# Local similarities in the pre-activation convolution chain: norms' rows in 8 transfers of twelve rows, batches of products in halves

## The chip, the cores and the metric

The kernel runs on one core of a Trainium2 chip. The metric is the device time of one execution in microseconds (us). The engines are named as in the profile: PE (matrix products), DVE (vector), ACT (scalar), POOL (GpSimd), SP (the queue that issues most transfers). ACTq and SPq are the queues in which ACT and SP issue transfers; 16 DMA engines carry them.

## The reference, cut to what matters

The input is 32 images of 32 channels, 56x56 pixels. Four residual stages follow each other, each on the input normalised per channel. The change lies in the second, local similarities:

```python
K, PAD, EPS = 5, 2, 1e-08
patches = _extract_patches(x)                       # 25 shifted copies, zero padded
dot = jnp.einsum('bchw,bckhw->bkhw', x, patches)    # product with each shift, summed over channels
norm_x = jnp.sqrt(jnp.sum(x * x, axis=1))
norm_p = jnp.sqrt(jnp.sum(patches * patches, axis=1))
sim = dot / jnp.maximum(norm_x[:, None] * norm_p, EPS)
weight = (sim + 1.0) * 0.5 * spatial_weight[None, :, None, None]
out = jnp.einsum('bckhw,bkhw->bchw', patches, weight)
```

The third stage is a gate per channel, and the fourth sorts, convolves and attends.

## The kernel before, in words

**Groups and rounds.** Four images with their 32 channels fill the 128 partitions: a group. The eight groups pass through a pipeline of rounds, from about 215 us to 2090 us of the span (the rest of the kernel isn't touched). In one round `a_vector` weighs and adds the shifts for group k ("taps"), and beside it `a_end_vector` finishes the group before, and `a_start_vector` prepares the next one: normalises it, makes the products of each pixel with its shifted neighbours, and turns them into similarities. The first round has no taps, the second has taps and a start but no end, six rounds (a hardware loop of three times two) have all three, and two last rounds start nothing. So eight rounds start a group. A round ends at a barrier of all engines (`end_round`, `close_round`), which SP closes.

**Steps.** By symmetry only 12 shifts (`HALF_TAPS`) are computed. With the centre there are 13 taps, and each image is done in two halves of 28 rows, so a round has 26 steps n. In step n DVE makes two weighted copies of the half image (L672, L676; `a_g`), PE adds them into PSUM with 8 + 8 products of 128x128 by 392 columns (L759, L763; `a_acc`), and DVE may be two steps ahead: step n waits for PE's step n - 2. The weights come back from DRAM (`simd`): for each step SP issues four loads (L520), each spreading one row over 32 partitions, into one of three buffers; the load for step n is issued when DVE has used the buffer, mostly after its step n - 3. After step 12 DVE reads the PSUM half out (L686), which PE's step 13 waits for, and after step 25 the other half.

**What a start does beside the steps.** DVE's step 5 normalises. ACT squares (L732), PE sums the squares over channels with 28 small products (L788) in its step 7, and ACT takes the root. DVE turns this into inverse norms in step 10 (L644 to L648, waits `a_nrm`, sets `a_nt`). PE transposes the two small results (L798) in its step 12, behind that step's dots, ACT copies them out (L746; `a_rt`), and then ACT issues the writes of the norms to `rnd` and `simd` (L704, L705), waits for them, and issues the loads of the norms' rows: for each of the 12 shifts one load into `rnc` (the norms) and one into `sim` (the norms shifted), each of 4 rows (one for each image) of 3136 floats, 24 loads in all (L711, L712; `a_rnl`). DVE's step 16 waits for all of them, multiplies (L654) and takes the similarity of the first half (L627, `a_sh`), which ACT stores (L720).

**Batches.** The products are made in six batches q: three for each half image (t = q modulo 3), each with four shifts j (`prd[0]` to `prd[3]`, DVE L619, 4 instructions). PE sums them over channels in `dots(q)` (L772, 32 products into PSUM). There is one set of `prd` buffers, so batch q waits for dots(q - 1) (`a_dot`). Before, batches 0 and 1 stand in steps 8 and 9, batch 2 in step 12, batches 3, 4 and 5 in steps 17, 18 and 20, similarities in steps 16 and 22, on PE the dots in the same steps.

Shift number m = 3j + t is in row 32j + 4t + image of `rnc` and `sim`.

Of the kernel before, what the change touches and what calls it, by code (L numbers as in the profile page):

```python
# [15 lines left out]
B, C, H, W = 32, 32, 56, 56  # L16
N = H * W
P = 128
TB = P // C
# [164 lines left out]
        assert not touched(first) & touched(ROW_LOTS[q - 1][1])  # L184
IMG_NET, IMG_PAIRS = placed(network(H))
TMP = max(max(n for _, _, n in ROW_NET), W * max(n for _, _, n in IMG_NET))
HALF_TAPS = [(0, 1), (0, 2)] + [(dh, dw) for dh in (1, 2) for dw in range(-2, 3)]


def tap(dh, dw):  # L190
# [3 lines left out]
def program(nc, x, wdct_t, keep, ident_in, same_batch, same_head, shifts, sw, gate_w, temp,  # L194
# [4 lines left out]
    with ctx:  # L199
# [7 lines left out]
        rnd = nc.dram_tensor("rnd", (TB * N + P,), f32).ap()  # L207
# [246 lines left out]
        a_tp, a_rt, a_rnw, a_rnl, a_sst = (sem(n, early) for n in ("a_tp", "a_rt", "a_rnw", "a_rnl", "a_sst"))  # L454
# [47 lines left out]


        PLACE = [n % 3 for n in range(2 * NS - 2)] + [1, 2]
        BEFORE = [max((m for m in range(n) if PLACE[m] == PLACE[n]), default=None) for n in range(2 * NS)]
        TURN = [max(m for m in range(2 * NS) if PLACE[m] == i) for i in range(3)]

# [15 lines left out]
        def a_sync(sp, end, start, k, taps=True, more=True):  # L523

            def end_out():
                sp.wait_ge(a_x3, 1)
                sp.dma_start(x3_t[end], xt[1 - k]).then_inc(a_st3, 16)

            def xp_out():
                sp.wait_ge(a_xp, 1)  # L530
                sp.dma_start(xpad_t[end], xp).then_inc(a_stp, 16)

            if start is not None:
                sp.dma_start(rnc, x_t[start]).then_inc(a_x, 16)
                for b in range(TB):
                    sp.dma_start(yt[C * b:C * b + 2, :], ydct_t[start, b]).then_inc(a_y, 16)
            for n in range(2 * NS):
                if taps and n >= 3:
                    sp.wait_ge(a_g, BEFORE[n] + 1)
                    s_load(sp, k, n)  # L540
                if end is not None and n == 8:
                    end_out()
                if end is not None and n == 10:
                    xp_out()
            if more:
                if start is not None:
                    sp.wait_ge(a_sst, 16 * 2 * NJ)
                for n in range(3):
                    if taps:
                        sp.wait_ge(a_g, TURN[n] + 1)  # L550
                    s_load(sp, 1 - k, n)
            if start is not None:
                sp.wait_ge(a_x, 16)
                sp.wait_ge(a_y, 16 * TB)
            if end is not None:
                sp.wait_ge(a_st3, 16)
                sp.wait_ge(a_stp, 16)
# [51 lines left out]
        def a_start_vector(chain, o, n):  # L609

            dve, link = chain.dve, chain.link

            def batch(q):
                h, t = divmod(q, NT3)
                if q:
                    dve.wait_ge(a_dot, q)
                for j in range(NJ):
                    dh, dw = HALF_TAPS[NT3 * j + t]
                    last = nc.vector.tensor_tensor(img3(prd[j]), rect(xn[o], HH * h + R1, HH, 0, 0),  # L619
                                                   rect(xn[o], HH * h + R1, HH, dh, dw), ALU.mult)  # L620
                last.then_inc(a_pr, 1)

            def similarity(h):
                dve.wait_ge(a_dot, NT3 * (h + 1))
                for i in range(4):
                    c = slice(HN * h + 392 * i, HN * h + 392 * i + 392)
                    last = nc.vector.scalar_tensor_tensor(out=sim[:, c], in0=sim[:, c], scalar=1e8,  # L627
                                                          in1=psum[:, 4 + i, 0:392], op0=ALU.min, op1=ALU.mult)
                last.then_inc(a_sh, 1)

            if n == 3:
                dve.wait_ge(a_x, 16)
                dve.wait_ge(a_y, 16 * TB)
                link(nc.vector.tensor_tensor(rnc, rnc, yt, ALU.add))
            if n == 4:
                chain.moments(rnc)
            if n == 5:
                chain.normalise(xi[o], rnc).then_inc(a_norm, 1)
                dve.wait_ge(a_norm, 1)
            if n in (8, 9):  # L640
                batch(n - 8)
            if n == 10:
                dve.wait_ge(a_nrm, 1)
                link(nc.vector.tensor_scalar_max(nr, nr, 1e-18))  # L644
                link(nc.vector.reciprocal(nr, nr))
                newton(link, nr, n2, nt)
                link(nc.vector.tensor_tensor(nt, nr, nr, ALU.mult))
                nc.vector.scalar_tensor_tensor(out=nt, in0=nt, scalar=1e8, in1=n2, op0=ALU.min,  # L648
                                               op1=ALU.mult).then_inc(a_nt, 1)
            if n == 12:  # L650
                batch(2)
            if n == 16:
                dve.wait_ge(a_rnl, 16 * 2 * NH)
                link(nc.vector.tensor_tensor(sim, rnc, sim, ALU.mult))  # L654
                similarity(0)
            if n in (17, 18):
                batch(n - 14)
            if n == 20:
                batch(5)
            if n == 22:  # L660
                similarity(1)

        def a_vector(dve, k, beside):

# [36 lines left out]
        def rn_scalar(act, k):  # L701

            act.wait_ge(a_rt, 2)
            act.dma_start(rnd[0:TB * N].rearrange("(r n) -> r n", n=TC), nrt).then_inc(a_rnw, 16)  # L704
            act.dma_start(simd[1 - k, NH].rearrange("b (k n) -> (b k) n", n=TC), ntt).then_inc(a_rnw, 16)  # L705
            act.wait_ge(a_rnw, 32)
            act.wait_ge(a_xc, 1)
            images = rnd[0:TB * N].rearrange("(b n) -> b n", n=N)
            for m, (dh, dw) in enumerate(HALF_TAPS):
                at = C * (m // NT3) + TB * (m % NT3)  # L710
                act.dma_start(rnc[at:at + TB, :], images).then_inc(a_rnl, 16)  # L711
                act.dma_start(sim[at:at + TB, :],  # L712
                              rnd[W * dh + dw:W * dh + dw + TB * N].rearrange("(b n) -> b n", n=N)).then_inc(a_rnl, 16)

        def sim_scalar(act, k):

            for h in range(2):
                act.wait_ge(a_sh, h + 1)
                for j in range(NJ):
                    act.dma_start(simd[1 - k, NT3 * j:NT3 * j + NT3, :, HN * h:HN * h + HN].rearrange("t b n -> (t b) n"),  # L720
                                  sim[C * j:C * j + ROWS_J, HN * h:HN * h + HN]).then_inc(a_sst, 16)
            act.wait_ge(a_sst, 16 * 2 * NJ)
# [28 lines left out]
        def a_tensor(pe, taps, ends, starts):  # L751
# [14 lines left out]

            def dots(q):
                t = q % NT3
                pe.wait_ge(a_pr, q + 1)
                for i in range(4):  # L770
                    for j in range(NJ):
                        last = nc.tensor.matmul(psum[C * j:C * j + C, 4 + i, 0:392], sel[:, t, :],  # L772
                                                prd[j][:, 392 * i:392 * i + 392], start=(t == 0), stop=(t == NT3 - 1),
                                                tile_position=(0, C * j))
                last.then_inc(a_dot, 1)

            for n in range(2 * NS):
# [6 lines left out]
                if starts:  # L784
                    if n == 7:
                        pe.wait_ge(a_sq, 1)
                        for i in range(NB):
                            last = nc.tensor.matmul(n2p.rearrange("p (b k) -> p b k", b=TB)[:, :, i],  # L788
                                                    sim[:, TC * i:TC * i + TC], ones4[:, 0::C], start=True, stop=True)
                        last.then_inc(a_n2, 1)  # L790
                        pe.wait_ge(a_n2e, 1)
                    if n in (8, 9):
                        dots(n - 8)
                    if n == 12:
                        dots(2)
                        pe.wait_ge(a_nt, 1)
                        for p, v in ((turnp[0], nr), (turnp[1], nt)):
                            last = nc.tensor.transpose(p, v, ident[0:TC, 0:TC])  # L798
                        last.then_inc(a_tp, 1)
                        pe.wait_ge(a_rt, 2)  # L800
                    if n == 17:
                        pe.wait_ge(a_sh, 1)
                    if n in (17, 18):
                        dots(n - 14)
                    if n == 20:
                        dots(5)

        def a_init(dve):

# [1218 lines left out]
```

## Time and profile before

| what | value |
|---|---|
| median of 3 runs | 15069.19 us (15061.56 to 15069.54) |
| profiled execution, its own time | 15071.54 us |
| its span, first to last instruction | 15070.0 us |
| mean granted PE clock | 0.713 of full speed |
| DVE busy over the span | 13765.0 us (91%) |
| DMA wait in front of L654, all 8 starts | 204.9 us |

The span is the time between the first and last instruction; 1.5 us lie around it. "Idle" is the time an engine stood still before an instruction, and the arrow names what ended it.

### The profile page before, as it was taken

How to read it: one execution, taken by the hardware profiler on the slowest of the kernel's cores; microseconds unless marked ns; L12 is line 12 of the kernel's file. 1: busy time of each engine (PE TensorE's matmuls, PEld its weight loads, DVE VectorE, ACT ScalarE, POOL GpSimd, SP SyncE). 2: the span in 40 equal slices, each digit the busy share in tenths (PEclk: the TensorE clock that was granted, in tenths of full speed). 3: DMA queues.
4: the chain of work that ended last, by engine and by line, in shares of the span. 5: the costliest groups of instructions: out<-in, count | busy, mean ns of one | idle time of the engine just before them, and what ended most of it. 6: DMA issues, size and time to landing. Idle time of an engine off the chain costs nothing. (4 is left out here: it accounts for less than half of the span.)

```text
span 15070.0 us, 121660 instructions
## 1 busy us (share of the span) xinstructions
PE 6719.5 (45%) x42188; PEld 2750.0 (18%) x42188; DVE 13765.0 (91%) x8241; ACT 7124.7 (47%) x6595; POOL 6003.7 (40%) x4372
## 2 busy tenths in 40 slices
PE   4777746480026525625714813833832015433310
PEld 2443422120012112211211201211211002111100
DVE  4777778899999999999999999999999999989978
ACT  0000013355565575565565566566566555444443
POOL 0000000066666666666666666666666640000000
PEclk8888878795558757857956956966866557666655
DMA  1455543210001001000100100100100001221232
GB/s 39 117 136 127 126 111 77 58 37 12 12 12 35 27 11 36 26 12 31 31 12 30 32 12 25 37 12 13 44 17 12 33 30 51 86 66 55 77 76 66
DMA packets 343162, 699.24 MB, mean 46 GB/s; under 512 B 71581, under 2 KB 275582, under 8 KB 331702
## 3 DMA queue, kind: packets, MB, share of 16 engines
q1 hardware_dynamic: 337398, 675.91, 16.6%
q10 hardware_dynamic: 5120, 15.26, 0.5%
q8 instruction: 342, 5.60, 0.2%
q14 instruction: 302, 2.47, 0.1%
HBM read 480.98 MB, written 209.95 MB: 46 GB/s over the span
## 5 line engine op out<-in xcount | busy, mean ns | idle before, releaser
L1197 DVE COPY_PREDICATED arena<-psum,arena 128x4096 f32<-128x4096 uint32 (+26 forms) x1456 | 4009.7, 2771 | 46.3 <-ACT psum L1157 45.9
L1204 DVE COPY_PREDICATED arena<-psum,arena 128x4096 f32<-128x4096 uint32 (+26 forms) x1456 | 3971.4, 2744 | 42.0
L1023 PE MATMUL psum<-arena,wt 128*32 128x448 f32 x31360 | 3217.1, 572 | 1248.2 <-DMA arena<-xpad 697.1
L1122 POOL TENSOR_TENSOR arena<-arena 128x1024 int32<-128x1024 int32 (+26 forms) x1456 | 2077.8, 1433 | 3063.7 <-DVE arena L1189 3060.3
L1108 POOL TENSOR_TENSOR arena<-arena 128x1024 bf16<-128x1024 f32 (+26 forms) x1456 | 1975.4, 1363 | 3223.7 <-SPq L267 3021.4
L1145 ACT ACTIVATE arena<-arena 128x4096 f32<-128x4096 f32 (+26 forms) x1456 | 3071.5, 2126 | 70.6 <-DVE arena L1204 37.9
L1165 ACT ACTIVATE masks<-psum 128x512 fp8e4<-128x512 f32 (+27 forms) x1256 | 923.1, 736 | 3566.7 <-DVE arena L1204 3565.5
L1114 POOL TENSOR_TENSOR arena<-arena 128x1024 int32<-128x1024 int32 (+26 forms) x1456 | 2005.7, 1384 | 0.0
L1023 PEld LDWEIGHTS psum<-arena,wt 128*32 128x32 f32 x31360 | 1038.2, 115 | 3429.7 <-issue 2321.6
L1413 PE MATMUL psum<-ident,arena 128*112 128x128 f32 x896 | 197.1, 385 | 2441.6 <-ACT arena L1332 1880.7
L1189 DVE TENSOR_TENSOR arena<-arena 128x1024 f32<-128x1024 f32 (+26 forms) x1456 | 1164.2, 813 | 99.7 <-POOL arena L1114 99.7
L1647 ACT ACTIVATE arena<-arena 128x2048 f32<-128x2048 f32 (+28 forms) x364 | 767.1, 2124 | 871.0 <-DVE arena L1680 869.2
L1682 DVE COPY_PREDICATED arena<-arena 128x2048 f32<-128x2048 uint8 (+28 forms) x364 | 974.0, 2692 | 76.5 <-ACT arena L1647 76.4
L1680 DVE COPY_PREDICATED arena<-arena 128x2048 f32<-128x2048 uint8 (+28 forms) x364 | 969.9, 2680 | 10.0
L1157 ACT ACTIVATE psum<-arena 128x512 f32<-128x512 bf16 (+10 forms) x1248 | 912.5, 731 | 0.0
L759 PE MATMUL psum<-arena 128*128 128x392 f32 x1664 | 669.7, 551 | 366.2 <-DVE arena L676 345.0
L1724 PE MATMUL psum<-masks,arena 128*128 128x512 fp8e4 (+3 forms) x992 | 326.5, 506 | 1104.0 <-DMA masks<-row_masks 633.8
L1457 PE MATMUL psum<-ident,arena 128*128 128x128 f32 x256 | 71.0, 433 | 1594.0 <-DVE arena L1391 1594.0
L1469 PE MATMUL psum<-arena 128*128 128x392 f32 x1024 | 572.2, 727 | 210.1 <-ACT arena L1324 78.8
L1413 PEld LDWEIGHTS psum<-ident,arena 128*112 128x112 f32 x896 | 155.1, 199 | 2498.7 <-ACT arena L1332 1891.7
L699 ACT ACTIVATE small<-small 128x1 f32<-128x1 f32 x24 | 4.9, 203 | 1209.4 <-DVE small L576 1209.4
L763 PE MATMUL psum<-arena 128*128 128x392 f32 x1536 | 543.3, 495 | 0.0
(132 smaller groups left out, 7662.0 us busy)
## 6 DMA issues: line engine op xcount, KB each, us to landing
arena<-xpad SPq DMA_DIRECT2D x896, 108.5 KB, 2.3
arena<-simd SPq DMA_DIRECT2D x416, 210.0 KB, 4.3
arena<-simd SPq DMA_DIRECT2D x416, 196.0 KB, 4.2
xpad<-arena SPq DMA_DIRECT2D x8, 1924.0 KB, 8.0
arena<-in_x SPq DMA_DIRECT2D x8, 1568.0 KB, 7.7
x3d<-arena SPq DMA_DIRECT2D x8, 1568.0 KB, 5.2
prodd<-arena SPq DMA_DIRECT2D x8, 1568.0 KB, 5.1
arena<-prodd SPq DMA_DIRECT2D x8, 1568.0 KB, 13.5
```

Of the source, the lines that this page charges most:

```text
L1023: last = nc.tensor.matmul(psum[C * b:C * b + C, n % C_BANKS, 0:CROWS * W], wt[:, g, C * w:C * w + C], cx[i % 2][b][:, y0:y0 + CROWS, x0:x0 ...
L1108: last = nc.gpsimd.tensor_tensor(packed_view(dbuf, here, piece, 1), lo, hi, ALU.subtract)
L1114: last = nc.gpsimd.tensor_tensor(packed_view(stmp, here, piece, 1), lo, hi, ALU.add)
L1122: last = nc.gpsimd.tensor_tensor(hi, packed_view(stmp, here, piece, 1), lo, ALU.subtract)
L1145: last = nc.scalar.activation(packed_view(ptmp, here, piece, NP), pair_views(pay[b], piece, NP)[0], ACT.Copy)
L1157: nc.scalar.activation(pmask[:, at:at + n], dbuf[:, here:here + n], ACT.Relu).then_inc(d_mw[k], 1)
L1165: last = nc.scalar.activation(masks[:, q % 4, lo:hi].bitcast(mybir.dt.float8e4), pmask[:, at:at + hi - lo], ACT.Sign, saturate=False)
L1189: last = nc.vector.tensor_tensor(lo, lo, hi, ALU.min)
L1197: last = nc.vector.copy_predicated(lo, wide_mask(q, k, piece, here), hi)
L1204: last = nc.vector.copy_predicated(hi, wide_mask(q, k, piece, here), packed_view(ptmp, here, piece, NP))
L1680: last = nc.vector.copy_predicated(hi, mask, packed_view(utmp, here, piece, NP))
L1682: last = nc.vector.copy_predicated(lo, mask, hi)
```

## The change

1. The order of `HALF_TAPS` changes, so that the three shifts of each j lie at equal distances. The loads of one j then go in one transfer of twelve rows, for `rnc` and for `sim`: 8 transfers. The source is a hand-written pattern, outermost three shifts (a step of 0 for `rnc`, of 56 or 1 floats for `sim`), then four images, then 3136 floats.
2. The inverse norms are computed in DVE's step 9, and PE transposes them in its step 9, ahead of dots(0).
3. A batch is made in two halves of two instructions in two steps (`BATCH`), and its dots come in the second of them. Similarities are in steps 16 and 23; step 15 has the wait for the norms' rows and L654.
4. SP's first three loads for the next round wait only for the stores of the first half of the similarities, and ACT's second four stores wait for the first four.

```diff
-HALF_TAPS = [(0, 1), (0, 2)] + [(dh, dw) for dh in (1, 2) for dw in range(-2, 3)]
+HALF_TAPS = [(dh, dw) for dw in (1, 2) for dh in range(3)] + [(dh, dw) for dh in (1, 2) for dw in range(-2, 1)]
...
+        BATCH = [(8, 9), (10, 11), (13, 14), (16, 17), (18, 19), (20, 21)]
+        SIMILAR = [16, 23]
...
-                    sp.wait_ge(a_sst, 16 * 2 * NJ)
+                    sp.wait_ge(a_sst, 16 * NJ)
...
-            def batch(q):
+            def batch(q, half):
...
-                for j in range(NJ):
+                for j in range(NJ // 2 * half, NJ // 2 * half + NJ // 2):
...
-            if n in (8, 9):
-                batch(n - 8)
-            if n == 10:
+            if n == 9:
                 dve.wait_ge(a_nrm, 1)
...
-            if n == 12:
-                batch(2)
-            if n == 16:
-                dve.wait_ge(a_rnl, 16 * 2 * NH)
+            if n == 15:
+                dve.wait_ge(a_rnl, 16 * 2 * NJ)
                 link(nc.vector.tensor_tensor(sim, rnc, sim, ALU.mult))
...
+            if n in SIMILAR:
+                similarity(SIMILAR.index(n))
+            for q, pair in enumerate(BATCH):
+                for half in range(2):
+                    if n == pair[half]:
+                        batch(q, half)
...
-            for m, (dh, dw) in enumerate(HALF_TAPS):
-                at = C * (m // NT3) + TB * (m % NT3)
-                act.dma_start(rnc[at:at + TB, :], images).then_inc(a_rnl, 16)
-                act.dma_start(sim[at:at + TB, :],
-                              rnd[W * dh + dw:W * dh + dw + TB * N].rearrange("(b n) -> b n", n=N)).then_inc(a_rnl, 16)
+            for j in range(NJ):
+                (dh, dw), (nh, nw) = HALF_TAPS[NT3 * j:NT3 * j + 2]
+                for dst, first, move in ((rnc, 0, 0), (sim, W * dh + dw, W * (nh - dh) + nw - dw)):
+                    act.dma_start(dst[C * j:C * j + ROWS_J, :],
+                                  bass.AP(rnd.tensor, rnd.offset + first, [[move, NT3], [N, TB], [1, N]])).then_inc(a_rnl, 16)
...
+                if h:
+                    act.wait_ge(a_sst, 16 * NJ)
...
-                pe.wait_ge(a_pr, q + 1)
+                pe.wait_ge(a_pr, 2 * q + 2)
...
-                    if n in (8, 9):
-                        dots(n - 8)
-                    if n == 12:
-                        dots(2)
+                    if n == 9:
                         pe.wait_ge(a_nt, 1)
                         for p, v in ((turnp[0], nr), (turnp[1], nt)):
                             last = nc.tensor.transpose(p, v, ident[0:TC, 0:TC])
                         last.then_inc(a_tp, 1)
                         pe.wait_ge(a_rt, 2)
...
+                    for q, (_, half) in enumerate(BATCH):
+                        if n == half:
+                            if q == NT3:
+                                pe.wait_ge(a_sh, 1)
+                            dots(q)
```

## Rows read from the trace of the kernel before

**Rows 1.** The page's first part: busy time, share, instructions of each engine.
```profile
PE 6719.5 (45%) x42188; PEld 2750.0 (18%) x42188; DVE 13765.0 (91%) x8241; ACT 7124.7 (47%) x6595; POOL 6003.7 (40%) x4372
```
**Rows 2.** Groups of instructions, 948.9 to 1173.8 us: busy, mean ns | idle before, releasers.
```profile
L672 DVE SCALAR_TENSOR_TENSOR arena<-arena 128x1568 f32<-128x1568 f32 x26 | 46.5, 1787 | 13.7 <-PE psum L763 8.2 <-issue 5.5
L772 PE MATMUL psum<-arena 128*32 128x392 f32 x192 | 17.0, 495 | 3.1 <-DVE arena L619 3.1
```
**Rows 3.** Line L654: duration ns min/median/max, first and last start; idle before it.
```profile
L654 DVE TENSOR_TENSOR arena<-arena x8: 3424/3424/3426, 300.0 to 1842.5; 128x3136 f32<-128x3136 f32 x8
  DMA arena<-rnd: 204.9, 8
```
**Rows 4.** Timeline of DVE, one loop round: start, us, instruction [idle before <-releaser].
```profile
1086.03 6.89 DVE L619 TENSOR_TENSOR arena<-arena 128x1568 f32<-128x1568 f32 x4
...
1102.98 6.90 DVE L619 TENSOR_TENSOR arena<-arena 128x1568 f32<-128x1568 f32 x4 [6.65 <-PE psum L772]
...
1113.20 0.21 DVE L644 TENSOR_SCALAR arena<-arena 112x112 f32<-112x112 f32 x1
...
1115.57 0.28 DVE L648 SCALAR_TENSOR_TENSOR arena<-arena 112x112 f32<-112x112 f32 x1
...
1173.84 3.42 DVE L654 TENSOR_TENSOR arena<-arena 128x3136 f32<-128x3136 f32 x1 [26.28 <-DMA arena<-rnd]
```
**Rows 5.** Timeline of PE in the same round.
```profile
1091.74 5.59 PE L759 MATMUL psum<-arena 128*128 128x392 f32 x8 [0.35 <-ACT arena L741]
1097.12 3.02 PE L763 MATMUL psum<-arena 128*128 128x392 f32 x8
...
1130.58 0.41 PE L798 MATMUL psum<-ident,arena 112*112 112x112 f32 x2
...
1138.53 2.79 PE L759 MATMUL psum<-arena 128*128 128x392 f32 x8
1141.16 2.80 PE L763 MATMUL psum<-arena 128*128 128x392 f32 x8
```
**Rows 6.** Timeline of ACT and its queue in the same round.
```profile
1131.02 0.42 ACT L746 ACTIVATE arena<-psum 112x112 f32<-112x112 f32 x2 [39.01 <-PE psum L798]
...
1136.95 0.25 ACTq L711 DMA_DIRECT2D arena<-rnd  x1
...
1144.84 0.32 ACTq L712 DMA_DIRECT2D arena<-rnd  x1
```
**Rows 7.** DMA queues, 305.3 to 310 us: four stores of twelve rows (6272 bytes).
```profile
DMA packets 96, 0.30 MB, mean 64 GB/s; under 512 B 48, under 2 KB 48, under 8 KB 96
```
**Rows 8.** DMA queues, 279 to 299 us: the row loads of the first round.
```profile
DMA packets 192, 1.21 MB, mean 61 GB/s; under 512 B 95, under 2 KB 95, under 8 KB 95
```
**Rows 9.** DMA queues, 1137 to 1153 us: row loads (q10) beside step loads (q1).
```profile
DMA packets 530, 2.54 MB, mean 159 GB/s; under 512 B 180, under 2 KB 180, under 8 KB 498
```
**Rows 10.** DMA queues, 1157 to 1169 us: DVE waits, and nothing new is issued.
```profile
DMA packets 151, 0.82 MB, mean 69 GB/s; under 512 B 65, under 2 KB 65, under 8 KB 109
q10 hardware_dynamic: 83, 0.53, 15.2%
q1 hardware_dynamic: 68, 0.30, 10.1%
```
**Rows 11.** Timeline of the first round (no taps), and L654 of the second.
```profile
247.62 4.48 PE L772 MATMUL psum<-arena 128*32 128x392 f32 x32 [0.35 <-ACT arena L741]
...
275.97 0.40 PE L798 MATMUL psum<-ident,arena 112*112 112x112 f32 x2
...
299.99 3.42 DVE L654 TENSOR_TENSOR arena<-arena 128x3136 f32<-128x3136 f32 x1 [28.44 <-DMA arena<-rnd]
...
347.43 5.41 SPq L520 DMA_DIRECT2D arena<-simd  x12
...
355.31 1.79 DVE L672 SCALAR_TENSOR_TENSOR arena<-arena 128x1568 f32<-128x1568 f32 x1 [12.39 <-SPq L267]
...
498.97 3.43 DVE L654 TENSOR_TENSOR arena<-arena 128x3136 f32<-128x3136 f32 x1 [27.45 <-DMA arena<-rnd]
```

More of the change, by code:

```diff
@@ L649, in a_start_vector @@
                                                op1=ALU.mult).then_inc(a_nt, 1)
-            if n == 12:
-                batch(2)
-            if n == 16:
-                dve.wait_ge(a_rnl, 16 * 2 * NH)
+            if n == 15:
+                dve.wait_ge(a_rnl, 16 * 2 * NJ)
                 link(nc.vector.tensor_tensor(sim, rnc, sim, ALU.mult))
[L655 to L661, printed above, removed]
+            if n in SIMILAR:
[4 more added lines that the diff above has]
+                        batch(q, half)
         def a_vector(dve, k, beside):
@@ L707, in rn_scalar @@
             act.wait_ge(a_xc, 1)
-            images = rnd[0:TB * N].rearrange("(b n) -> b n", n=N)
-            for m, (dh, dw) in enumerate(HALF_TAPS):
-                at = C * (m // NT3) + TB * (m % NT3)
-                act.dma_start(rnc[at:at + TB, :], images).then_inc(a_rnl, 16)
-                act.dma_start(sim[at:at + TB, :],
-                              rnd[W * dh + dw:W * dh + dw + TB * N].rearrange("(b n) -> b n", n=N)).then_inc(a_rnl, 16)
+            for j in range(NJ):
[3 more added lines that the diff above has]
+                                  bass.AP(rnd.tensor, rnd.offset + first, [[move, NT3], [N, TB], [1, N]])).then_inc(a_rnl, 16)
         def sim_scalar(act, k):
@@ L800, in a_tensor @@
                         pe.wait_ge(a_rt, 2)
[L801 to L806, printed above, removed]
+                    for q, (_, half) in enumerate(BATCH):
[3 more added lines that the diff above has]
+                            dots(q)
         def a_init(dve):
```

## The prediction, made before the changed kernel ran

> **What bounds the kernel now.** I read the page first: DVE is busy for 13765 of 15070 us [rows 1], so only DVE's own stops, or work taken off it, are worth anything. The change takes no instruction off DVE. Next the groups of instructions of one loop round: DVE's copies L672 have waited 8.2 us for PE in all [rows 2]. The line view then finds the one large stop: L654, the product with the norms' rows, has waited 204.9 us for the loads from `rnd`, 8 times, 25.6 us a time [rows 3]. The timelines of a round show why. PE transposes the norms at 1130.6, ACT issues the loads from 1136.95 to 1145.2, and DVE, idle for 26.3 us, goes on at 1173.84 [rows 4 to 6]. So the loads take 36.9 us from the first issue, 28.7 us after the last one. The issues themselves aren't the bound.
>
> **Why the loads are slow.** A packet view counts data rows and small closing packets. The 24 loads of the first round leave 96 rows and some 95 packets under 512 B, four for each load [rows 8]; the four stores of twelve rows leave 48 and 48, twelve for each [rows 7]. So a transfer closes once on each engine it uses, and four-row loads use four of 16, always few at once: q10 and q1 together hold 15.2 + 10.1 = 25.3% of 16 engines, four of them, full, while DVE waits [rows 10]. Each of the four carries 24 rows. In the first round, alone, that takes from 279 to 299.99, less 1.3 us for start and landing, 19.7 us or 0.82 us a row [rows 8, 11]. From 1137 to 1153 there are 530 - 498 = 32 rows, 8 an engine, 2.0 us each, beside 498 - 180 = 318 rows of step loads, 20 an engine [rows 9]. From 1157 to 1169 there are 42 rows, 10.5 an engine, 1.14 us each, beside 44 rows of step loads that four engines still owe, one for one [rows 10]. A few engines with two queues are the bottleneck.
>
> **The change, part by part.** I put it on the clock of this round.
>
> *Norms earlier.* DVE now makes half of batch 0 in step 8 (2 x 1.7 = 3.4 us, half of 6.9, from 1086.0 to 1089.4), step 9's copies to 1092.9, then the norms (2.6 us, from L644 at 1113.20 to the end of L648 at 1115.8 [rows 4]) and the other half. PE's sums of squares end at 1091.4, step 8's accumulation takes 8.2 us at the lower clock and step 9's 5.3 (2 x 2.63) [rows 5]: 1105.2, transposes 1105.7, copies out by 1106.2, where it was 1131.4 [rows 6]. Norms leave 25.2 us earlier. With the same 5.5 us for the write [rows 6], the loads are issued from 1111.7, the first row starts near 1112.3.
>
> *Where DVE asks for them.* dots(0) now come behind the transposes and end at 1109.0 (2.8 us, 17.0 / 6) [rows 2], so half 1 of batch 1 waits 5.6 us and step 10's copies 1.2 us for the accumulation; batch 1 had waited 6.65 us [rows 4]. Then DVE goes on in steps of 3.4 + 3.4 us: step 11 to 1119.5, step 12 to 1121.2, the half read-out waits 2.0 us for PE's step 12 and ends at 1129.1, steps 13 and 14 end at 1139.3, step 15's copies at 1142.7. There L654 stands now. The rest (17 us of products, similarities, PE-bound last steps) is the same work; the halves of batches 4 and 5 wait 1.6 us each for dots, two waits of 1.9 to 2.2 us in steps 15 and 16 go. Over the round the small waits grow by 12.2 - 11.4 = 0.8 us. If no row load were late, a loop round would save its stop less that: the six have (204.9 - 28.4 - 27.4) / 6 = 24.8 (the second round's is 27.4) [rows 3, 11], so 24.0, and the second 26.6.
>
> *8 transfers for 24.* 16 issues of 0.35 us go from ACT's queue [rows 6], where nothing waits for them: nothing. What counts is engines. The destination still counts twelve rows outermost, but the new source counts three shifts outermost. In the rows above the number of engines equals the outermost count of both sides, four and twelve [rows 7, 8]; no transfer of the trace has sides that differ. Equal shares along both outermost counts give three engines, and I take that; twelve is the other bound. On three, 96 rows are 32 an engine, not 24. The packing thus makes the loads longer.
>
> The Trainium skill, "DMA: Bandwidth & Descriptors" ("Why a DMA increments its semaphore by 16 and not by 1"), says that a transfer is cut over the largest number of engines up to 16 that divides the outermost counts of both sides, and its rules for kernel authors warn of a small outermost dimension. By that rule it is three here, and the four and twelve above agree.
>
> *The wait that is left.* There are 1142.7 - 1112.3 = 30.4 us for 32 rows. Lower bound, the rate of the first round without step loads: 32 x 0.82 = 26.2 us, hidden. Upper bound, the rates of the round itself: DVE doesn't stop now, so step loads come on (five between 1112 and 1143, 40 rows an engine, as dense as before), 15 rows at 2.0 us, and 17 at 1.14 once DVE stands: 19.4 us, landed at 1161.9, a wait of 19.2 us. The step loads are there, so I stay near the upper: 16 us, a little less because a share now closes once for four rows. A part of it may show as DVE's copies (L672) waiting for a late step load, since three engines hold those up too; it is the same time.
>
> *First round.* No step loads, no taps. PE's sums end before 247.6, so norms from 248, transposes at 251 for 275.97 [rows 11], loads from 253.7; 26.2 us, landed at 280.6 where it was 300.0: 19 us. At its end SP's 12 loads (5.4 us, 347.43) stood between the last stores and the barrier [rows 11]; they now wait for first-half stores only: 5 us. In full rounds the same wait was covered by PE-bound steps. Together 24 us.
>
> *Sum.* 24 + (26.6 - 16) + 6 x (24.0 - 16) = 83 us. The profiled execution took 15071.5 us (1.5 around the span), 2.3 above the median of the runs. 15071.5 - 83 = 14988.5, by the median 14986.
>
> **Rivals.**
> *Hidden (0.20).* The rows go over twelve engines, or four rows in a line go so much faster that 30.4 us are enough. For: the stores of twelve rows did use twelve engines [rows 7]. 24 + 26.6 + 6 x 24 = 195 us saved, 14874. The skill page's rules also say to put many small transfers into one large one; by that rule this rival would win, but the row loads' time lies behind the last issue [rows 4, 6], which speaks against issue cost.
> *Slower or no gain (0.08).* The step-load rows queued on the three engines keep all 32 rows at 2.0 us [rows 9]: 64 us, landed at 1176.3, a wait of 33.6 us in seven rounds, 24 - 7 - 6 x 9.6 = 41 us lost, 15110. It decides from a wait of 195 / 7 = 27.8 us, or 1.8 us a row. Against: the rate was 1.14 as soon as DVE stood [rows 10].
> *The forecast (0.72):* exposed by 5 to 23 us.
>
> **How the numbers follow.** What this measurement can tell from no change is about 0.2%, 30 us. The upper bound above gives 24 + 7.4 + 28.8 = 60 us saved, 15009; if the dense rate outlasts DVE's stop by some 8 us, 3.5 us more in each of seven rounds, near 15030. The lower end takes in the hidden case, 14874 less a few: 14866. Within that range I see 0.9; the forecast's own range is 14915 to 15030. Savings under 30 us need a wait above 23.5 us, all in the second rival: same 0.05, slower 0.03, faster 0.92.
>
> **What would show it.** In the packet view of a round's row loads: 24 closing packets for 96 rows (96 if twelve engines). L798 some 25 us earlier in the round. L654 still waiting for `rnd` in seven rounds, about 16 us, nearly none in the first; or L672 waiting for DMA from `simd` in step 15. With twelve engines no wait at L654 at all. A gain in the first round unlike 24 us, or new waits for L772 above 1.6 us, would say that my steps are misplaced.

## The result, and the profile after

The changed kernel takes 14888.53 us (median of 4 runs, 14887.01 to 14903.87), the kernel before 15068.69 (4 runs beside it): ratio 0.9884, 95% interval 0.9867 to 0.9901. It is faster by 180 us, where 83 were forecast; that lies 97 us below the forecast and 14.5 us above the time of the first rival (hidden, 14874). The profiled execution took 14887.01 us.

The page's first part, engine by engine:

```profile
span 14884.8 us, 121541 instructions
PE 6707.4 (45%) x42188; PEld 2746.4 (18%) x42188; DVE 13771.3 (93%) x8241; ACT 7130.0 (48%) x6595; POOL 6008.9 (40%) x4372
```

DVE does the same work (13771 us against 13765 in [rows 1]) in a span 185 us shorter: the whole gain is idle time of DVE. The line view of L652, which was L654 [rows 3], says whose:

```profile
L652 DVE TENSOR_TENSOR arena<-arena x8: 3415/3418/3420, 278.3 to 1644.6; 128x3136 f32<-128x3136 f32 x8
its engine sat idle before it (us, times) until:
who waited for it (us, times):
```

Nothing stands between the second line and the third: all eight waits for `rnd`, 204.9 us before, are gone. Nor did they turn into late step loads. DVE's copies (L669, before L672) waited for `simd` 9.1 us in the whole kernel:

```profile
L669 DVE SCALAR_TENSOR_TENSOR arena<-arena x208: 1781/1791/1795, 329.8 to 1864.6; 128x1568 f32<-128x1568 f32 x104
its engine sat idle before it (us, times) until:
  PE psum L761: 82.8, 48
  SPq L267: 21.0, 6
  issue: 11.1, 2
  DMA arena<-simd: 9.1, 7
```

The same loop round as in [rows 4], by DVE's timeline (start, us, instruction, [idle before <-releaser]):

```profile
984.31 3.48 DVE L621 TENSOR_TENSOR arena<-arena 128x1568 f32<-128x1568 f32 x2
...
991.12 0.21 DVE L644 TENSOR_SCALAR arena<-arena 112x112 f32<-112x112 f32 x1
...
1007.33 3.49 DVE L621 TENSOR_TENSOR arena<-arena 128x1568 f32<-128x1568 f32 x2 [5.28 <-PE psum L770]
...
1025.49 1.98 DVE L683 TENSOR_TENSOR arena<-arena,psum 128x392 f32<-128x392 f32 x4 [2.04 <-PE psum L757]
...
1031.84 1.79 DVE L669 SCALAR_TENSOR_TENSOR arena<-arena 128x1568 f32<-128x1568 f32 x1 [0.96 <-DMA arena<-simd]
...
1042.06 3.42 DVE L652 TENSOR_TENSOR arena<-arena 128x3136 f32<-128x3136 f32 x1
```

PE and ACT's queue in it, answering to [rows 5, 6]:

```profile
1003.55 0.36 PE L793 MATMUL psum<-ident,arena 112*112 112x112 f32 x2
1004.42 2.84 PE L770 MATMUL psum<-arena 128*32 128x392 f32 x32 [0.51 <-ACT arena L744]
```
```profile
1003.95 0.42 ACT L744 ACTIVATE arena<-psum 112x112 f32<-112x112 f32 x2 [13.35 <-PE psum L793]
...
1008.67 3.59 ACTq L708 DMA_DIRECT2D arena<-rnd  x5
```

From the start of the first batch to the transposes it is 1003.55 - 984.31 = 19.2 us (1130.58 - 1086.03 = 44.6 before): 25.3 us earlier in the round, 25.2 were forecast. From the first issue of a row load to L652 it is 33.4 us, in which DVE never stops for rows. An issue of the new form takes 3.59 / 5 = 0.72 us, not 0.35, and nothing waited for it.

Now the engines. In the first round nothing but row loads runs, and the queue view from 254 to 271 us answers to [rows 8]:

```profile
DMA packets 116, 1.19 MB, mean 70 GB/s; under 512 B 21, under 2 KB 21, under 8 KB 21
q10 hardware_dynamic: 116, 1.19, 17.5%
```

95 rows and 21 closing packets, where the kernel before had 95 of the latter. (24 closings are due, three for each of 8 transfers; the window cuts some off.) The queue's 17.5% of 16 engines is 2.8 engines busy all through. So the transfers run on three engines, as forecast, with 32 rows each. The packet records of q10 give the time from the first row's start to the last row's end:

| | rows / closings an engine | first round, alone | beside step loads |
|---|---|---|---|
| before, 24 transfers | 24 / 24 | 19.6 us | 34.6 to 36.6 us |
| after, 8 transfers | 32 / 8 | 16.0 us | 26.1 to 27.3 us |

More rows on fewer engines were faster. The records also give each packet's own duration. In the first round a row lasts 0.73 us on average before and 0.50 us after; beside step loads 0.85 to 0.95 before and 0.64 to 0.67 after. No row of any run is shorter than 0.47 us. A closing lasts 0.01 to 0.03 us on average in every run, at most 0.09. The queue views say the same of the rows: from 279 to 299 us of the kernel before, q10 holds 22.4% of 16 engines, 0.75 us for each of 96 rows, and 17.5% of 17 us above is 0.50 us for each of 95:

```profile
q10 hardware_dynamic: 191, 1.20, 22.4%
```

In the loop round the step loads pass at the same time: from 1009 to 1036 us the queue of step loads holds 39.0% of the 16 engines.

```profile
q1 hardware_dynamic: 530, 2.39, 39.0%
q10 hardware_dynamic: 115, 1.18, 14.7%
```

Last, the first round (start of what [rows 11] shows), with the late end of the round:

```profile
247.91 0.22 DVE L644 TENSOR_SCALAR arena<-arena 112x112 f32<-112x112 f32 x1 [10.70 <-ACT arena L741]
...
278.33 3.42 DVE L652 TENSOR_TENSOR arena<-arena 128x3136 f32<-128x3136 f32 x1
...
329.77 1.79 DVE L669 SCALAR_TENSOR_TENSOR arena<-arena 128x1568 f32<-128x1568 f32 x1 [6.94 <-SPq L267]
```

L652 starts at 278.33 here without a wait for rows. These had landed at 271.5, and what DVE waited for on the way were the norms (10.70 us above) and the dots (5.07 and 5.57 us before L621). The first L669 starts at 329.77 instead of 355.31: 25.5 us. The second round's stands at 519.29, 189.5 later (216.5 before): 27.0 us. The six loop rounds take 200.6 us each and took 223.8: 23.2 each, 139 in all. That makes 191.7. The first instruction of the next stage (L953, before L959) starts at 1929.0 instead of 2120.2, 191.2 us earlier. At the end of the span 185.2 are left; the missing 6 us arise in stages that the change doesn't touch and are smaller than the scatter of the runs.

### The profile page after: what moved, and what is told of

It reads as the page before. It is cut to its first block and busy times, and to the rows that moved or that the text cites. A ratio compares the mean times of both kernels' runs of the same rounds, so it can differ in the third digit from the quotient of the medians.

```text
span 14884.8 us, 121541 instructions
## 1 busy us (share of the span) xinstructions
PE 6707.4 (45%) x42188; PEld 2746.4 (18%) x42188; DVE 13771.3 (93%) x8241; ACT 7130.0 (48%) x6595; POOL 6008.9 (40%) x4372
```

## The experiments

Two theories of the gain stood after the result. **A:** a transfer closes with a packet on each engine it uses, that packet costs about as much as a row while step loads run, and 8 closings an engine for 24 is why 32 rows pass in 26.5 us. From 24 rows with 24 closings (35.1 us: 1.46 a pair) and 8 groups of four rows with one closing (26.5 us: 3.31 a group), a row costs (3.31 - 1.46) / 3 = 0.62 us and a closing 0.85; the experiments use 0.61 and 0.86. From 19.6 and 16.0 us of the first round, without step loads, the same equations give 0.39 and 0.42. This is a fit of two prices to two totals, and the packets' own durations above speak against it as a price of the closing packet; the runs below say how far it carries. **B:** the transfers' form matters little; the rows are hidden because the norms leave 25 us earlier. Later two more came up, on the halves of the batches: **C**, that they cost waits, and **D**, that they don't (experiment 5 gives both letters a narrower meaning).

The kernels of experiments 1 to 4 stand beside 12 runs of the kernel before (median 15073.42), those of 5 to 8 beside 9 others (15079.97). Between these groups, and with the changed kernel, ratios are compared, or the time at which the next stage begins in the trace.

**1. The changed kernel with 24 transfers of four rows again.**

```diff
-            for j in range(NJ):
-                (dh, dw), (nh, nw) = HALF_TAPS[NT3 * j:NT3 * j + 2]
-                for dst, first, move in ((rnc, 0, 0), (sim, ...)):
-                    act.dma_start(dst[C * j:C * j + ROWS_J, :], ...)
+            for m, (dh, dw) in enumerate(HALF_TAPS):
+                at = C * (m // NT3) + TB * (m % NT3)
+                act.dma_start(rnc[at:at + TB, :], images).then_inc(a_rnl, 16)
+                act.dma_start(sim[at:at + TB, :], ...).then_inc(a_rnl, 16)
```

> The changed kernel with the norms' rows in 24 loads of four rows again, all else as changed. Theory A (a load's closing packet on each engine is what made a row cost 1.5 us; in threes of engines with four rows to a closing it costs 0.8): the rows take some 35 us as before, DVE asks for them after some 31, so L652 waits about 4 to 5 us in seven rounds, 14889 + 32 = about 14920 us. Theory B (the row rate rose because the new order of the round leaves the DMA engines freer): 24 rows an engine at 0.82 us, 20 us, no wait, 14889 us.

Measured: 14932.95 us (14922.94 to 14952.25), ratio 0.9909 (0.9894 to 0.9924). The rows took 35 to 39 us, 22.6 in the first round, with 96 closings. The next stage begins at 1976.7 us, 47.7 later than in the changed kernel. The wait shows mostly where the prediction had said that a part of it might, at DVE's copies, though a step earlier: 6.43 us in step 14 of one loop round, not in step 15. L652 waits little, and the copies L669 wait for the step loads, which the same engines carry:

```profile
  DMA arena<-rnd: 4.4, 6
```
```profile
  PE psum L762: 82.7, 49
  DMA arena<-simd: 46.1, 13
```

(4.4 us is L652's line, the two others are L669's; in the changed kernel they were none, 82.8 and 9.1.) So B is wrong: packing is worth 48 us by the start of the next stage, and 40 by the medians, each set against the kernel before beside it. A had 14920, so the cost is somewhat above its number, and most of it falls on the step loads, for which DVE asks first.

**2. The kernel before with the 8 transfers alone**: the new `HALF_TAPS` and the new loads, nothing else.

> The kernel before with only the loads in 8 transfers of twelve rows (and the order of shifts that this needs). Theory A: the rows take 26 to 27 us after the first one instead of 35, L654 waits 8.7 us less in seven rounds and 3.6 less in the first, 15069 - 65 = about 15004 us. Theory B: three engines with 32 rows at 1.5 us, 48 us, the wait grows by 12 us a round, about 15155 us. Either way 24 closing packets for 96 rows.

Measured: 15032.56 us (15017.61 to 15038.78), ratio 0.9971 (0.9961 to 0.9982). The rows took 25.4 to 30.1 us, 16.2 in the first round, and L654 waits 155.9 us for them, 49 less than in [rows 3]; A had 15004, 29 us better, B 15155:

```profile
  DMA arena<-rnd: 155.9, 8
```

The next stage begins at 2078.1, 42 us earlier. My forecast was that packing on three engines makes the loads longer; here it stands alone and makes them shorter, in every round. With the packing worth 42 to 48 us in either kernel, the other 143 to 149 of the 191 us come with the rest of the change: experiment 1, which has everything but the packing, reaches the next stage 143.5 us before the kernel before. That rest is the earlier norms, the moved batches and SP's wait (experiment 6); no run has the earlier norms alone. It took both parts to bring the wait to nothing.

**3. The changed kernel with half-width rows**, 16 transfers for 8, the same three engines and bytes.

```diff
-                    act.dma_start(dst[C * j:C * j + ROWS_J, :],
-                                  bass.AP(..., [[move, NT3], [N, TB], [1, N]])).then_inc(a_rnl, 16)
+                    for c in (0, HN):
+                        act.dma_start(dst[C * j:C * j + ROWS_J, c:c + HN],
+                                      bass.AP(..., [[move, NT3], [N, TB], [1, HN]])).then_inc(a_rnl, 16)
```

> The changed kernel with each load of twelve rows cut into two of half the columns: 16 transfers, the same bytes, twice the closings (16 an engine) and twice the data packets (64 of 6272 bytes an engine). Theory A with closings alone: 8 more closings at some 0.86 us, rows done after 33 us, L652 waits 2 to 3 us in seven rounds, about 14907 us. If only the bytes count: unchanged 14889. If each packet, large or small, takes its turn with a step-load packet: some 45 us, a wait of 14 us, about 14990.

Measured: 14907.85 us (14900.91 to 14912.49), ratio 0.9889 (0.9874 to 0.9904). The rows took 31.7 to 34.7 us beside step loads, with 48 closings; 32 x 0.61 + 16 x 0.86 = 33.3 is what A gives. The bytes alone would have left 26.5, and a cost for each packet of any kind far more. L652 waits 28.6 us in all, and the next stage begins 21 us later:

```profile
  DMA arena<-rnd: 28.6, 7
```

By time alone the run wouldn't tell (the intervals of the ratios overlap); the packets and the wait do. Beside step loads A's two prices come out to within 1.6 us. In the first round, where nothing else runs, they don't: 32 x 0.39 + 16 x 0.42 = 19.2 us, and the half rows took 16.4, 0.4 more than the whole rows of the changed kernel (255 to 273 us):

```profile
DMA packets 240, 1.20 MB, mean 67 GB/s; under 512 B 48, under 2 KB 48, under 8 KB 240
q10 hardware_dynamic: 240, 1.20, 17.1%
```

So eight more closings an engine, and twice the packets, cost next to nothing alone and 7 us beside step loads. The run doubles three things at once (closings, row packets and transfers), so it can't give the 7 us to the closings. The records point elsewhere. Where q10's packet ends and no other of q10 starts at once, its engine has broken off from q10. In the changed kernel's loop rounds that happens after 35 to 44 of 96 rows and 9 to 13 of 24 closings; here after 67 to 88 of 192 and 20 to 24 of 48. (The records don't name the engine, so these counts go by the times alone.) The breaks double, and most of them stand behind rows. The step loads are denser here too, with 16 rows a us for 14.

**4. The changed kernel with whole batches.** The batches' dots had cost the changed kernel waits before L621 (25 of them), as they had the kernel before (81.3 us in 13):

```profile
L621 DVE TENSOR_TENSOR arena<-arena x192: 1781/1785/1794, 233.7 to 1692.6; 128x1568 f32<-128x1568 f32 x192
its engine sat idle before it (us, times) until:
  PE psum L770: 80.6, 25
```

```diff
-        BATCH = [(8, 9), (10, 11), (13, 14), (16, 17), (18, 19), (20, 21)]
+        BATCH = [(9, 9), (11, 11), (14, 14), (17, 17), (19, 19), (21, 21)]
```

> The changed kernel with each batch made whole in the second step of its pair (9, 11, 14, 17, 19, 21), dots and all else in the same steps. Theory C (the halves cost: half 0 of the next batch asks for dots one step too early, so DVE waits for PE): a schedule laid out from the rows gives 6 us a round less in seven rounds, about 14845 us; the wait of 5.3 us before step 10's half goes. Rival D (the halves spread DVE's work and so keep DVE and PE from waiting for each other): 10 to 40 us slower than the changed kernel, 14900 to 14930 us, with longer waits for L770.

Measured: 14836.98 us (14832.66 to 14845.18), ratio 0.9843 (0.983 to 0.9857), the next stage from 1888.7 us, 40.3 earlier.

```profile
L621 DVE TENSOR_TENSOR arena<-arena x192: 1778/1783/1794, 250.6 to 1652.7; 128x1568 f32<-128x1568 f32 x192
its engine sat idle before it (us, times) until:
  PE psum L770: 19.4, 4
```

61 us of waits before L621 went, and some came back: L652 waits 10.4 us for rows again, L644 for the norms 40.9 instead of 16.9. C holds for these places: the halved batches as placed cost 40 us against whole ones a step later by the start of the next stage, 52 to 56 by the medians. The dots need both halves, so a first half one step ahead brings PE nothing; it asks for the `prd` buffers a step sooner and waits there for the dots of the batch before (the 5.28 us above; at the same batch the whole version doesn't wait).

**5. Five batches whole, at later places.**

```diff
+        BATCH = [(9, 9), (11, 12), (14, 14), (18, 18), (20, 20), (22, 22)]
```

> The changed kernel with five of the six batches of products whole, at (9,9), (11,12), (14,14), (18,18), (20,20), (22,22). Theory C (a batch must lie where the shifted copy it displaces is not the one TensorE waits for; where a half costs VectorE a wait for TensorE, it is the place that costs, not the halving by itself): working out each round's order of waits from the durations of the profile after gives 9.7 us a round less than the changed kernel, over seven rounds 68 us, so 14820 us; the second batch stays in halves and must not bring the waits back. Theory D (whole batches gain because they are whole): five of six whole gives five sixths of the 51.5 us that six gave, so 14846 us.

Measured: 14860.72 us (14856.94 to 14864.28), ratio 0.9854 (0.9839 to 0.9869). C's 14820 is missed by 41 us. The next stage begins at 1900.6 us, 12 after that of experiment 4. Against experiment 4, DVE saves 20 us of waits at the read-outs L683 (43.1 for 62.8), and spends 23 more where the rows are due:

```profile
  DMA arena<-rnd: 33.8, 7
```

Here L652 is asked for earlier and the rows, in 27 to 30 us, bound it again; L669's waits for PE grew by 7 us as well. My working had taken the rows as hidden at a fixed time. D's arithmetic (14846) is nearer, but 20.2 us of waits are left before L621, about as with all six whole (19.4), though one batch is halved here; so nothing speaks for the halving as such being the cost. The schedule by places is no better than its row-load term.

**6. The changed kernel with SP's wait put back** (`sp.wait_ge(a_sst, 16 * 2 * NJ)`).

> The changed kernel with one thing put back: SyncE waits for all of the step's stores of the similarities, 16*2*NJ, before it loads on, and not for 16*NJ. If that wait is hidden behind the rows of norms, the time stays at 14889 us within 10. If it holds the first load of the next round's step, it costs up to 6 us in the first round and less in the others: 14894 to 14925 us.

Measured: 14901.44 us (14894.53 to 14905.61), ratio 0.9881 (0.9866 to 0.9896), no different from the changed kernel's. In the trace the second round starts its copies at 334.6 us, not 329.8: 4.8 us, as the first round's term had it (5). The next stage begins 18.9 us later in this one execution, with L669, L621 and L644 each waiting 2 to 8 us more; whether the loop rounds pay too stays open, since the runs don't show it.

**7. Norms still earlier.** The sums of squares two steps earlier on PE (n == 5), their root on ACT ahead of the copy of the normed rows, norms and transposes in step 8.

```diff
-        BATCH = [(8, 9), (10, 11), (13, 14), (16, 17), (18, 19), (20, 21)]
+        BATCH = [(7, 8), (10, 10), (12, 12), (18, 18), (20, 20), (22, 22)]
...
-            if n == 9:
+            if n == 8:
                 dve.wait_ge(a_nrm, 1)
...
-                    if n == 7:
+                    if n == 5:
                         pe.wait_ge(a_sq, 1)
...
-                    if n == 9:
+                    if n == 8:
                         pe.wait_ge(a_nt, 1)
```

> The changed kernel with the sums of squares two steps earlier on TensorE, their root on ScalarE ahead of the copy of the normed rows, the norms one step earlier on VectorE and TensorE, and the batches at (7,8), (10,10), (12,12), (18,18), (20,20), (22,22). Theory C, by the same working as for the late places: 1.4 us a round less than those, over seven rounds 10 us, so 14810 us, and the idle time of VectorE at the read of the norms (2.7 us a round in that working) gone. Rival: the sums meet TensorE while it is behind, and the time stays at that of the late places, 14820 us, or above.

Measured: 14824.55 us (14824.03 to 14830.65), ratio 0.9833 (0.9819 to 0.9846): the fastest of the study, 14.6 us above what C gave. L652 waits for nothing and L644 in the first round alone. The step loads pay part of it. The row loads now take 31.5 to 32.8 us with the same 32 rows and 8 closings an engine, where A gives 26.4; 17 rows of step loads a us start beside them, in the changed kernel 14:

```profile
  PE psum L761: 73.0, 34
  DMA arena<-simd: 43.1, 21
```

**8. The same with the norms written three times,** so that the four loads of `rnc` go over twelve engines, a row each.

```diff
-            act.dma_start(rnd[0:TB * N].rearrange("(r n) -> r n", n=TC), nrt).then_inc(a_rnw, 16)
+            for c in range(NT3):
+                act.dma_start(rnd[TB * N * c:TB * N * c + TB * N].rearrange(...), nrt).then_inc(a_rnw, 16)
...
+                act.dma_start(rnc[C * j:C * j + ROWS_J, :],
+                              rnd[0:NT3 * TB * N].rearrange("(r n) -> r n", n=N)).then_inc(a_rnl, 16)
```

> As the kernel with the sums early, but the norms are written three times, so that the four loads of rnc take rows on twelve engines, a row each; the four of sim stay on three. On those three engines 20 rows and 8 closings stand for 32 rows and 8 closings. Theory A (0.61 us a row and 0.86 us a closing beside the step loads): the last row lands after 19 us and not 26.5. If the rows are fully hidden already, the time is that of the kernel with the sums early, 14810 us, within 10; two more stores of 12 packets and 12 x 4 closings may cost the step loads up to 5 us. If the three loaded engines still hold the step loads up by a few us a round, it gains those: 14780 to 14800 us.

Measured: 14840.71 us (14835.07 to 14855.97), ratio 0.9841 (0.9827 to 0.9854). The rows land 6 us earlier than in experiment 7, after 25.5 to 28.2 us, with 60 closings, and not after 19. Nothing is gained: the next stage begins 20.1 us later than in experiment 7. DVE's timeline shows what a late load before the half's read-out does. At 1008.52 DVE waits for a step load, and then at 1021.53 for PE, whose step 13 had to wait for the read-out L683:

```profile
1008.52 1.79 DVE L669 SCALAR_TENSOR_TENSOR arena<-arena 128x1568 f32<-128x1568 f32 x1 [4.28 <-DMA arena<-simd]
...
1011.94 1.97 DVE L683 TENSOR_TENSOR arena<-arena,psum 128x392 f32<-128x392 f32 x4
...
1021.53 1.79 DVE L669 SCALAR_TENSOR_TENSOR arena<-arena 128x1568 f32<-128x1568 f32 x1 [4.22 <-PE psum L764]
```
```profile
1013.96 4.79 PE L760 MATMUL psum<-arena 128*128 128x392 f32 x8 [6.24 <-DVE arena L683]
```

L669's waits for PE are 101.0 us in all against 73.0, those for `simd` 35.0 against 43.1.

In its first round, alone, the rows took 16.9 us on twelve engines, where three took 16.0 to 16.4. The queue view from 255 to 273 us:

```profile
q10 hardware_dynamic: 156, 1.20, 32.5%
```

That is 5.2 engines busy on average instead of 2.8, for the same rows in the same time. Each row lasted 0.96 us on average, and up to 1.93.

**A's prices against all the rounds,** in us:

| kernel | rows / closings an engine | alone: A, measured | beside step loads: A, measured |
|---|---|---|---|
| 1, four-row loads | 24 / 24 | 19.4, 22.6 | 35.3, 35.0 to 39.4 |
| 2, packing alone | 32 / 8 | 15.8, 16.2 | 26.4, 25.4 to 30.1 |
| 3, half rows | 32 (as 64 halves) / 16 | 19.2, 16.4 | 33.3, 31.7 to 34.7 |
| 7, norms earlier | 32 / 8 | 15.8, 16.4 | 26.4, 31.5 to 32.8 |
| 8, twelve engines | 20 / 8 | 11.2, 16.9 | 19.1, 25.5 to 28.2 |

Beside step loads A comes within 4 us in experiments 1 to 3 and is 5 to 9 us too low in 7 and 8. Alone it is 3 to 6 us off in 1, 3 and 8, and its 0.39 us for a row alone is less than the shortest row of any run (0.47). In the changed kernel's first round 32 rows at 0.50 fill the 16.0 us by themselves, and a row that follows a closing starts 6 ns after it. What is shown is that the form matters: eight transfers of twelve rows pass faster than 24 of four. That the closing packets are what costs is not shown, and alone it is refuted.

A rival that no run here tests fits the first rounds better: a limit at the place that the rows come from or go to. The rows of a four-row load lie in four neighbouring partitions, those of a twelve-row load in twelve. Alone, the forms with twelve rows moved the 1.20 MB at 71 to 76 GB/s, on three engines or on twelve, and the four-row loads at 61 and 53. Rows last up to 1.75 us in the kernel before, 2.01 in experiment 1 and 1.93 here, some four times the shortest; in the changed kernel's first round only 5 of 96 pass 0.55.

## Why the prediction was wrong, by its own steps

**What held.** *DVE's stops are the kernel's time*: yes. *Norms leave 25.2 us earlier*: 25.3. *Half 1 of batch 1 waits 5.6 us, the half's read-out 2.0*: 5.28 and 2.04. *Three engines*: 24 closings for 96 rows. *First round 24 us*: 25.5, its SP term 5: 4.8. *If no row load were late, 26.6 and 24.0 a round*: 27.0 and 23.2. Every term but one came out within 2 us a round. In the first round part of that is luck: my 19 us at L654 stood on rows that land at 280.6, and they landed at 271.5. L652 starts at 278.3 because DVE waited for the norms and the dots, which saves 21.7. The Trainium skill, "DMA: Bandwidth & Descriptors" ("Why a DMA increments its semaphore by 16 and not by 1"), gave the three engines, and the trace agrees: 24 closings, 2.8 engines busy.

**The step that failed** is *the wait that is left*, 16 us in each of seven rounds, 112 us of which nothing came. Its engine count was right and its rate was wrong. I took 2.0 and 1.14 us a row from the kernel before [rows 9, 10], where each load gave one row to each of four engines, and used them for 32 rows an engine in 8 loads, with "a little less because a share now closes once for four rows". The form of the loads was the main thing. 32 rows took 26.5 us beside step loads, 0.83 us a row, not the 46.4 that leave a wait of 16. There were 30.4 us by my steps and 31.9 by the trace, from the first row at 1010.2, 1.5 us after its issue and not 0.6, to L652 at 1042.06. Even the lower bound I named, 26.2 us for a round without step loads, was not one: there the same rows took 16.0, 0.50 us a row instead of 0.82. The 2.0 itself was 1.8, since the window begins 1.4 us ahead of the first row. (Step 8's accumulation is 8.4 us in [rows 5] and not 8.2, which changes nothing.) Why a row of the old form is dearer stays open: the experiments show the form's worth, and their own theory of it, the closings, fails in the first rounds.

**The rival that came true** was put down to twelve engines or to "four rows in a line go so much faster". It was the second, at 0.20. Against it I had only said that issue cost isn't the bound, which is right and says nothing of how long a row takes in another form. The Trainium skill's advice in the same page ("Rules for kernel authors") to put many small transfers into one large one held, then, and experiments 1 and 2 give it 42 to 48 us here, for another reason than issue. The Trainium skill's same page, "Queues, rings and completion order", says that the semaphore's write lands only behind the engine's earlier writes, across its queues. No run here tests that; the closings' own records, 0.01 to 0.03 us on average, show no engine held by it.

**The halves** had only the term of 0.8 us a round and needed no more for the sum: the waits before L621 are 80.6 us, and 81.3 before. Experiments 4 and 7 show that they, or the places they lead to, left 40 to 59 us lying by the start of the next stage; experiment 7 moves the norms too.

**How the 191 us divide.** Packing alone 42 (experiment 2), and 48 when taken away last (experiment 1). The rest, 143 to 149, comes with the earlier norms, the moved batches and SP's wait (4.8 us in the first round).

## What to carry to other kernels

A rate read from a trace belongs to the form of the transfers in it: how many rows each gives to each engine, over how many engines, and beside what. Before a rate is used for another form, look in the trace for a stretch with that form; where there is none, the rate is one bound of the range and not its middle. And before a cost fitted to two totals is called the price of a packet, look at how long the packets themselves last, and try it on the quietest stretch: here the fit gave a closing 0.42 us alone, its record lasts 0.01, and doubling the closings there cost 0.4 us for all eight.

When engines are shared by two queues, an overload shows at whichever wait comes first, not at the loads that cause it: with 24 transfers again, 37 of 48 us stood before loads that hadn't been touched. And a wait that is removed hands its time to the next resource only as far as that one's slack reaches: so work out each due time anew after every shift of places.

## What the runs showed of the hardware

- A row of 12544 bytes lasted 0.47 us at the least and 0.50 on average when only eight twelve-row loads ran, on three engines; with 24 four-row loads on four engines it was 0.73. Beside step loads the averages were 0.64 to 0.67 and 0.85 to 0.95. A closing packet (4 bytes) lasted 0.01 to 0.03 us on average, at most 0.09.
- Three engines with 32 rows in 8 loads took 26.1 to 27.3 us beside step loads, four with 24 rows in 24 loads 34.6 to 36.6. Alone it was 16.0 for 19.6.
- Cutting each load into two of half rows cost 0.4 us alone and some 7 us beside step loads.
- The issue of a four-row load from a two-level source takes ACT's queue 0.35 us, that of a twelve-row load from a two-level source about 0.5 (experiment 8), that of a twelve-row load from a three-level source 0.7 to 0.8.
- Alone, twelve engines for half of the rows took 16.9 us, three for all of them 16.0. In experiment 8 the rows came in after 25.5 to 28.2 us and the kernel was 16 us slower than experiment 7's.
